# Grouped attention in a 12-layer float32 decoder: dividing the probabilities before their turn, and value products with the values as weights

## The reference, cut to what matters

```python
def _L1_attn_ref(hidden_states, Wq, Wk, Wv, Wo):
    q = (hidden_states @ Wq.T).reshape(B, S, 16, 64).transpose(0, 2, 1, 3)
    k = (hidden_states @ Wk.T).reshape(B, S, 4, 64).transpose(0, 2, 1, 3)
    v = (hidden_states @ Wv.T).reshape(B, S, 4, 64).transpose(0, 2, 1, 3)
    k, v = jnp.repeat(k, 4, axis=1), jnp.repeat(v, 4, axis=1)
    scores = jnp.einsum('bhqd,bhkd->bhqk', q, k) * 64 ** -0.5
    scores = scores + causal[None, None]
    probs = jax.nn.softmax(scores, axis=-1)
    out = jnp.einsum('bhqk,bhkd->bhqd', probs, v)
    return out.transpose(0, 2, 1, 3).reshape(B, S, 16 * 64) @ Wo.T
...
x = _layernorm(x + _L1_attn_ref(x, L1_attn_Wq, L1_attn_Wk, L1_attn_Wv, L1_attn_Wo), axis=-1)
```

## Time and profile before

| | us |
|---|---|
| Median of 3 runs (lowest, highest) | 4686.77 (4686.62, 4692.56) |
| The profiled execution, its own time | 4658.31 |
| Its span | 4656.5 |
| TensorE, VectorE busy | 3992.7, 3324.2 |
| ScalarE, GpSimd busy | 2208.0, 1392.6 |
| First fill to last aggregate of the L1a stage | 1331.2 to 1987.2 |

### The profile page before, as it was taken

One profiled execution on the slowest core, in us unless ns is written; L12 is line 12 of the kernel. 1 busy time (PEld: TensorE's weight loads), 2 busy tenths in 40 slices (PEclk: granted clock), 3 DMA queues, 4 the chain that ended last, 5 costly groups with the idle time before them and its releaser, 6 DMA issues. The chain is left out here.

```text
span 4656.5 us, 142989 instructions
## 1 busy us (share of the span) xinstructions
PE 3992.7 (86%) x51849; PEld 2927.6 (63%) x51890; DVE 3324.2 (71%) x7831; ACT 2208.0 (47%) x3967; POOL 1392.6 (30%) x2469
## 2 busy tenths in 40 slices
PE   8997997999989999889899561799998968879986
PEld 6775666565667877767677441577675434447765
DVE  7986883555557777678788316788786767759985
ACT  4554552222224344356588133455784345545543
POOL 5653341000000000012245505233222234435543
PEclk9998996999999999999999585899998978889998
DMA  2011111000000000011000252000111200000001
GB/s 72 27 46 36 38 36 35 11 14 10 10 13 1 0 0 0 1 41 44 29 17 17 66 149 63 12 13 13 32 33 43 57 7 0 0 12 23 23 17 36
DMA packets 184580, 127.91 MB, mean 27 GB/s; under 512 B 43056, under 2 KB 175408, under 8 KB 184112
## 3 DMA queue, kind: packets, MB, share of 16 engines
q1 hardware_dynamic: 168128, 110.62, 8.0%
q0 software_dynamic: 4096, 8.40, 0.6%
q10 hardware_dynamic: 12144, 6.03, 0.4%
HBM read 77.24 MB, written 18.35 MB: 21 GB/s over the span
## 5 line engine op out<-in xcount | busy, mean ns | idle before, releaser
L920 DVE TENSOR_TENSOR L0f_SG<-L0f_SG,L0f_psY 128x512 f32<-128x512 f32 x176 | 120.6, 685 | 219.5 <-PE L0f_psY L849 219.0
L888 ACT ACTIVATE L0f_SG<-L0f_psY 128x512 f32<-128x512 f32 x176 | 105.1, 597 | 357.1 <-PE L0f_psY L847 357.1
L860 PEld LDWEIGHTS L0f_psO<-L0f_W,L0f_G 128*128 128x128 f32 x1408 | 182.2, 191 | 101.5 <-issue 61.9
L860 PE MATMUL L0f_psO<-L0f_W,L0f_G 128*128 128x128 f32 x1408 | 188.3, 277 | 17.1 <-DVE L0f_G L924 10.9
L2351 POOL TENSOR_TENSOR L1a_rs<-L1a_ag,eps 128x1 f32<-128x1 f32 x64 | 12.1, 189 | 593.9 <-DVE L1a_ag L2521 593.9
L847 PE MATMUL L0f_psY<-L0f_XT,L0f_W 128*128 128x512 f32 x352 | 182.1, 599 | 0.7 <-ACT L0f_G3T L876 0.7
L849 PE MATMUL L0f_psY<-L0f_XT,L0f_W 128*128 128x512 f32 x352 | 180.6, 595 | 2.3 <-issue 0.2
L1531 POOL TENSOR_TENSOR L0f_rt<-L0f_ag,eps 128x4 f32<-128x4 f32 x16 | 3.2, 200 | 513.5 <-DVE L0f_ag L1525 513.5
L2461 ACT ACTIVATE L1a_PR<-L1a_PR 128x1024 f32<-128x1024 f32 x64 | 67.6, 1056 | 150.5 <-DVE L1a_PR L2482 150.5
L2443 PE MATMUL L1a_psO<-L1a_WO,L1a_OT 128*128 128x128 f32 x1024 | 133.7, 285 | 2.9 <-DVE L1a_OT L2497 2.6
L2443 PEld LDWEIGHTS L1a_psO<-L1a_WO,L1a_OT 128*128 128x128 f32 x1024 | 122.3, 196 | 20.0 <-issue 16.8
(11 more groups left out here) (647 smaller groups left out, 12914.8 us busy)
## 6 DMA issues: line engine op xcount, KB each, us to landing
L1m_WB<-in_w12b SPq DMA_DIRECT2D x23, 321.0 KB, 3.3
L1m_BUF<-sorted_x SPq DMA_DIRECT2D x23, 256.0 KB, 3.6
sorted_y<-L1m_BUF ACTq DMA_DIRECT2D x23, 256.0 KB, 3.8
L0a_CS<-in_ctx SPq DMA_DIRECT2D x32, 128.0 KB, 2.1
KB<-L0a_KT SPq DMA_DIRECT2D x128, 32.0 KB, 1.8
L0x_CS<-in_ctx SPq DMA_DIRECT2D x32, 128.0 KB, 2.1
L0x_CR<-in_ctxT SPq DMA_DIRECT2D x32, 128.0 KB, 2.3
KB<-L0x_KT SPq DMA_DIRECT2D x128, 32.0 KB, 1.8
```

Of the source, the lines that this page charges most:

```text
L860: m = nc.tensor.matmul(psO[:, j, :], G[:, gb, 0, j * P:(j + 1) * P], W2[:, k, :], start=k == 0 and j == 0, stop=k == NCH - 1, skip_group_c ...
L888: nc.scalar.activation(SG[:, yb, :], psY[:, yb, 0, :], ACT.Silu).then_inc(S["silu"].sem, 1)
L920: nc.vector.tensor_tensor(SG[:, yb, :], SG[:, yb, :], psY[:, yb, 1, :], ALU.mult).then_inc(S["product"].sem, 1)
```

## The change

The probabilities are divided by their sum on VectorE, in place, right behind the reciprocal (new `nc.vector.tensor_tensor` on PR). Their turn waits for that and moves on TensorE from the front of the slot to behind the scores and the fills of place 0; the value products move behind place 1. In them the values are the weights now and the turned probabilities of four heads stream, 256 columns at a time; each sequence s has a PSUM bank, and the result has features on partitions, which is what the projection needs. So ON, its multiplication and its turn are gone, and OT is copied straight from psQ, one sequence by ScalarE, the other by VectorE. Head pairs of the second sequence lie the other way round on partitions, so WO is loaded a second time with its halves swapped. The projection is done for each sequence by itself: 16 matmuls on 64 columns of the array instead of 8 on 128. A line near the top advances counters of the first stage's semaphores.

```diff
                             nc.vector.tensor_scalar(MF[:, M.u, :], MI[:, M.u, :], 0.0, None, ALU.not_equal).then_inc(S["mask_used"].sem, 1)
...
+            S.advance(dict(rows_rest=16 * MORE, weights_rest=32), arrive)
             S.advance(dict.fromkeys(("xs", "rstd", "var_eps", "out_rows", "f_tx", "f_k", "f_q", "f_v", "o_tx", "o_k", "o_q", "o_v"), PAIRS))
             S.advance(dict.fromkeys(("scores", "shifted", "maxed", "probs", "pt_a", "pt_b", "turned_a", "turned_b", "pv", "normed",
                                      "recip", "ot", "o_turned", "proj", "res", "bn", "stats"), TILES))
...
-            WO = mem.sb("WO", [P, QC, D])
+            WO = mem.sb("WO", [P, 2, QC, D])
...
             PR, PT = mem.sb("PR", [P, 2, HEADS, SEQ]), mem.sb("PT", [P, QC, P])
...
-            ON, OT = mem.sb("ON", [P, QC, P]), mem.sb("OT", [P, QC, P])
+            OT = mem.sb("OT", [P, 2, QC, SEQ])
...
             psP, psO = mem.pb("psP", [P, 2, 4, P]), mem.pb("psO", [P, 2, 4, P])
             psJ = psO[:, 0, 0, :]
-            psH = psO.rearrange("p r c (e d) -> p r (c e) d", d=GD)
+            psQ = psO.rearrange("p s c (e q) -> p s (c e) q", q=SEQ)
...
-                    for d, s_ in ((WQ[:, :, :], io["wq"]), (WK[:, :, :], io["wk"]), (WV[:, :, :, :], io["wv"]), (WO[:, :, :], io["wo"])):
+                    for d, s_ in ((WQ[:, :, :], io["wq"]), (WK[:, :, :], io["wk"]), (WV[:, :, :, :], io["wv"]), (WO[:, 0, :, :], io["wo"]), (WO[0:64, 1, :, :], io["wo"][64:128]), (WO[64:128, 1, :, :], io["wo"][0:64])):
                         sp.dma_start(d, s_).then_inc(S["weights_in"].sem, 16)
-                    sp.wait_ge(S["weights_in"].sem, S["weights_in"].base + 64)
-            S.advance(dict(weights_in=64))
+                    sp.wait_ge(S["weights_in"].sem, S["weights_in"].base + 96)
+            S.advance(dict(weights_in=96))
...
             def copy_out(eng, N, n):
...
                     def slot(T):
                         A = T - 1
-                        if A.ok:
-                            pe.wait_ge(S["probs"].sem, S["probs"].base + A.t + 1)
-                            for hb, free, done in ((0, S["ot_a"], S["turned_a"]), (1, S["ot_b"], S["turned_b"])):
-                                if after(A.t):
-                                    pe.wait_ge(free.sem, free.base + A.t)
-                                for j in range(4):
-                                    b = hb * 4 + j
-                                    m = nc.tensor.transpose(psP[:, hb, j, :], PR[:, A.par, 2 * b:2 * b + 2, :].rearrange("p h k -> p (h k)"), ident)
-                                m.then_inc(done.sem, 1)
                         if T.ok:
...
                             copied(pe, T.p, NFILL - 1)
...
                         fills(T, 0)
                         if A.ok:
...
+                            pe.wait_ge(S["normed"].sem, S["normed"].base + A.t + 1)
+                            for hb, free, done in ((0, S["pt_a"], S["turned_a"]), (1, S["pt_b"], S["turned_b"])):
+                                if after(A.t):
+                                    pe.wait_ge(free.sem, free.base + A.t)
+                                for j in range(4):
+                                    b = hb * 4 + j
+                                    m = nc.tensor.transpose(psP[:, hb, j, :], PR[:, A.par, 2 * b:2 * b + 2, :].rearrange("p h k -> p (h k)"), ident)
+                                m.then_inc(done.sem, 1)
+                        fills(T, 1)
+                        if A.ok:
                             pe.wait_ge(S["pt_a"].sem, S["pt_a"].base + A.t + 1)
                             pe.wait_ge(S["pt_b"].sem, S["pt_b"].base + A.t + 1)
                             if after(A.t):
                                 pe.wait_ge(S["res"].sem, S["res"].base + A.t)
                             pace(pe, S)
-                            for c in range(QC):
-                                for r in range(2):
-                                    half_ = slice(64 * r, 64 * r + 64)
-                                    for s in range(2):
-                                        m = nc.tensor.matmul(psH[64 * s:64 * s + 64, r, c, :], PT[half_, c, 64 * s:64 * s + 64],
-                                                             VT[half_, A.u, 2 * A.par + s, c // 4, :], start=True, stop=True)
+                            for g4 in range(2):
+                                for s in range(2):
+                                    for r in range(2):
+                                        half_, o = slice(64 * r, 64 * r + 64), r if s == 0 else 1 - r
+                                        m = nc.tensor.matmul(psQ[64 * o:64 * o + 64, s, 4 * g4:4 * g4 + 4, :], VT[half_, A.u, 2 * A.par + s, g4, :],
+                                                             PT[half_, 4 * g4:4 * g4 + 4, 64 * s:64 * s + 64], start=True, stop=True)
                             m.then_inc(S["pv"].sem, 1)
-                        fills(T, 1)
-                        if A.ok:
-                            pe.wait_ge(S["normed"].sem, S["normed"].base + A.t + 1)
-                            for hb, done in ((0, S["o_turned_a"]), (1, S["o_turned_b"])):
-                                for j in range(4):
-                                    m = nc.tensor.transpose(psP[:, hb, j, :], ON[:, 4 * hb + j, :], ident)
-                                m.then_inc(done.sem, 1)
                         fills(T, 2)
                         if A.ok:
                             pe.wait_ge(S["ot_a"].sem, S["ot_a"].base + A.t + 1)
                             pe.wait_ge(S["ot_b"].sem, S["ot_b"].base + A.t + 1)
                             for c in range(QC):
-                                m = nc.tensor.matmul(psJ, OT[:, c, :], WO[:, c, :], start=c == 0, stop=c == QC - 1)
+                                for s in range(2):
+                                    m = nc.tensor.matmul(psJ[64 * s:64 * s + 64, :], OT[:, s, c, :], WO[:, s, c, :], start=c == 0, stop=c == QC - 1, skip_group_check=True)
                             m.then_inc(S["proj"].sem, 1)
...
                             nc.scalar.activation(PR[:, T.par], PR[:, T.par], ACT.Exp, scale=scale).then_inc(S["probs"].sem, 1)
                         copies(act, T, 1)
                         if A.ok:
-                            act.wait_ge(S["o_turned_a"].sem, S["o_turned_a"].base + A.t + 1)
+                            act.wait_ge(S["pv"].sem, S["pv"].base + A.t + 1)
                             if after(A.t):
                                 act.wait_ge(S["proj"].sem, S["proj"].base + A.t)
-                            nc.scalar.activation(OT[:, 0:4, :], psP[:, 0], ACT.Copy).then_inc(S["ot_a"].sem, 1)
+                            nc.scalar.activation(OT[:, 0, :, :], psQ[:, 0], ACT.Copy).then_inc(S["ot_a"].sem, 1)
                         copies(act, T, 2)
...
                             nc.vector.tensor_tensor(PR[:, T.par].rearrange("p (c r) k -> p r c k", r=2), psS[:, :, :, :],
                                                     mx[:, T.par, :].rearrange("p (r c) -> p r c", r=2).unsqueeze(3).to_broadcast([P, 2, QC, SEQ]), ALU.subtract).then_inc(S["shifted"].sem, 1)
                         copies(dv, T, 0)
+                        copies(dv, T, 1)
                         if A.ok:
                             dv.wait_ge(S["pv"].sem, S["pv"].base + A.t + 1)
-                            dv.wait_ge(S["recip"].sem, S["recip"].base + A.t + 1)
-                            if after(A.t):
-                                dv.wait_ge(S["o_turned_b"].sem, S["o_turned_b"].base + A.t)
-                            nc.vector.tensor_tensor(ON[:, :, :].rearrange("p c (r d) -> p r c d", d=GD), psH,
-                                                    rden[:, A.par, 1, :].rearrange("p (c r) -> p r c", r=2).unsqueeze(3).to_broadcast([P, 2, QC, GD]), ALU.mult).then_inc(S["normed"].sem, 1)
-                        copies(dv, T, 1)
-                        if A.ok:
-                            dv.wait_ge(S["o_turned_b"].sem, S["o_turned_b"].base + A.t + 1)
                             if after(A.t):
                                 dv.wait_ge(S["proj"].sem, S["proj"].base + A.t)
-                            nc.vector.tensor_copy(OT[:, 4:8, :], psP[:, 1]).then_inc(S["ot_b"].sem, 1)
+                            nc.vector.tensor_copy(OT[:, 1, :, :], psQ[:, 1]).then_inc(S["ot_b"].sem, 1)
                         copies(dv, T, 2)
                         if T.ok:
...
                             nc.vector.tensor_reduce(rden[:, T.par, 0, :], PR[:, T.par], AX, ALU.add).then_inc(S["summed"].sem, 1)
                             dv.wait_ge(S["summed"].sem, S["summed"].base + T.t + 1)
                             nc.vector.reciprocal(rden[:, T.par, 1, :], rden[:, T.par, 0, :]).then_inc(S["recip"].sem, 1)
+                            dv.wait_ge(S["recip"].sem, S["recip"].base + T.t + 1)
```

(3 more changed lines are left out.)

## The result

| | median us | ratio to before, same chip |
|---|---|---|
| before | 4686.62 | |
| changed | 4700.15 | **1.0027** (95%: 1.0018 to 1.0036) |

13.5 us slower, where 4694 was forecast: inside the range and inside the likeliest case's own 4683 to 4706. At 0.27% it is just over the 0.2% that the forecast had called no change, a part of that case to which it gave a chance of 0.04. Measured again on another chip, the ratio was 1.0032 (1.0022 to 1.0043).

A forecast was written before the change was run, and what follows sets the result against it. TensorE's order was taken to bound the attention stage, 19.96 us a pair. Work and waits -20 us and clock falls +27 made +7: 4665 in the profiled execution's terms, 4694 with 28 us added for the runs' median; range 4662 to 4724.

The forecast's parts named there:

- likeliest case: Whole kernel: 10 to 18 clock falls of 1.6 to 2.2 us in the attention stage, 4683 to 4706 us; chance 0.42.
- thin stretches: Even slots, scores' end to K fill: about 4.0 us in which TensorE only turns ten blocks, 1.4 us busy.
- Work removed and swapped: Attention pair: ON's turn and waits gone, 3.0 us; value products 1.0 a block, projection 2.04, multiplication 1215 ns on probabilities.
- The X fill's wait: Even slot, TensorE waiting for GpSimd's XS copy behind VectorE's longer chain: 1.6 us where it was 0.4.
- The K fill's wait: Even slot, TensorE waiting for XT, which ScalarE copies behind both PT copies: a new wait of 1.1 us.
- Work and waits in the stage: Attention stage: pairs 19.4 us instead of 19.96, 17 us, plus 5 at the end: -22 us.
- The clock: Even slots of attention: clock falls in about 45 to 50% of pairs, 14 of 30, 1.9 us each, +27 us.
- The copies of WO: In front of the attention stage: two more copies of half of WO, 1.9 us, once, not covered.
- B: Attention stage: the clock holds, under 5 falls, leaving the gain of 20 us, 4666 us; chance 0.33.
- C: Attention stage: the clock falls in nearly every pair, 30 x 1.9 - 20 = +37, 4724 us; chance 0.13.
- D: Value products lose their overlap, both row halves writing one PSUM bank: 2.0 us a block, +44, 4731 us; chance 0.12.

The follow-up runs named there:

- XS early: The changed kernel with GpSimd's XS copy one slot earlier, in front of the wait for the aggregate: 0.9840 of the kernel before, 4581 us.
- XT first: The changed kernel with only ScalarE's XT copy moved in front of the two PT copies, XS staying late: 0.9861 of the kernel before.

## Why the prediction was right, point by point

Both new waits, their sizes and the clock's falls behind about half of the thin stretches are as forecast. That the stage's own sum came out almost exact is luck: it was 5 us longer by the forecast (-22 by work and waits, +27 by the clock) and is 4.9 longer, but the two terms are -31.5 and +36.

- **Work removed and swapped.** The turn of ON went. Value products 1.02 us a block (1.0 said), projection 1.90 (2.04 said, 0.14 too dear), multiplication 1225 ns (1215 said).
- **The X fill's wait**: 1.6 us said, 1.64 measured. VectorE's chain 4.2 said, 4.31 measured. The step said that the wait came from that chain's new 1.1 us and from the turn gone from the front; without the division 1.13 us are left. Only 0.5 us is the division's, since behind it the aggregate is held by the projection. The size was right, the reason only in part.
- **The K fill's wait**: 1.1 said, 1.03 measured.
- **Work and waits in the stage**: -22 us said (17 in the pairs, 5 at the end). With the clock held by added matmuls it is -31.5: a pair takes 19.3 us where it took 19.9, 19 us in 30 pairs, and the end, from the last X fill on, 40.0 where it took 51.7, 12 us. The end is the term that was too small. The sum left out that the old kernel's own two falls there, which the prediction itself prices at 2.6 and 1.6 us, would go with the waits that made them. For the whole kernel -20 us said and -20 measured (0.9957, interval -28 to -12) agree only because of what the start and the stages behind give back.
- **The clock.** 14 falls of 1.9 us, +27, were said. There were 17, and they cost 2.1 us each, 36 us. Taking the share of the pairs by the stretch's place between 3.3 and 4.76 us gave 45 to 50%; it was 17 in 30, 57%. Over the experiments the share does rise with the stretch: none of 30 at 2.3 us (XS early) or 2.8 us (XT first), 7 at 3.5 (without the division), 17 at 4.0. But inside the changed kernel length doesn't tell the stretches apart: all but the first are 3.96 to 4.12 us long, and in the steady part the clock falls behind three of five, in the same order throughout, with some that keep it no shorter than those that lose it. What decides there is open, so that the share came out near is in part luck too.
- **The copies of WO** in front of the stage: 1.9 us said, 4.0 measured in both profiles of the changed kernel. The rate of the four copies before didn't hold for six: the two pieces of 64 partitions took 6.9 us to land.
- **Not foreseen**: the stage behind (L1x), untouched, took 320.7 and 320.6 us in the two profiles of the changed kernel, 317.4 and 317.9 in the two of the old one. Its clock is low for 27 us instead of 21. That is at most a part of it: with the four matmuls added its clock is low for 21 us, and it still takes 319.6. The cause is open. In sum: 4.9 (stage) + 4.0 (copies) + 3.3 (behind) + 1.3 (L1f, not seen again in the second profile) = 13.5 us, the other stages, which differ by up to 1.3 us, left out. So the step from the +7 that was forecast to +13.5 is the copies, 2 us, and the two stages behind, 4.6, which the forecast had at nothing; it isn't the clock.
- **Rivals.** B (the clock holds) is what the kernel with added matmuls shows, not the changed one. C (nearly every pair) is out: 17 of 30. D (no overlap of the value products) is out: both row halves write one bank of psO at 1.02 us a block, as fast as the old form on two banks; its 16 instructions start in groups of four, 0.02 us from first to last, and 0.2 to 0.3 us from group to group. The Trainium skill, TensorEngine Tiling (Array Packing), Gotcha 1: PSUM Pressure, says that different row tiles cannot access one bank at the same time; on different partitions of it the measurement shows no cost, and it decides. The other rule of the Trainium skill, TensorE: Matmul & The Clock Gate, Part 4: PE-mode transpose, that a transpose doesn't count as TensorE being busy in the same way, is contradicted for the clock by the stretch filled with turns, where 3 of the 17 falls were left.

## What to carry to other kernels

When a step is moved on one engine, lay out what stands in front of each wait anew: here a turn that had hidden a GpSimd copy and a ScalarE copy moved behind both, and what is a 2.3% gain with two copies issued earlier was a 0.3% loss without. A wait on TensorE costs more than its length where it makes a stretch thin, since the clock may fall behind it; the granted clock of the stage and the duration of the first matmuls behind a wait show that, and work put into the wait tells it apart from the wait itself. A copy that only reads should not stand behind another tile's wait on an in-order engine.

## What the runs showed of the hardware that was not expected

- Behind a stretch of about 4.0 us with 1.4 us of transposes in it the clock fell in 17 of 30 pairs, to a granted 0.50 (1.2 GHz), for 2.1 us of lost time each; with 1.0 us of matmuls more in the same stretch, never; with 1.0 us of transposes more, in 3.
- The loss is in the rows right behind the wait: K fills of 2.08 us instead of 1.13, while the 32 recorded instructions of the projection, 5.4 us after the K fill's start, were at full speed (1.97 us).
- The two pieces of a weight on 64 partitions each (256 KB) took 6.9 us to land (median) behind 1.25 MB, longer than the whole weight (512 KB) in front of them with 5.2. How much of that is the queue in front and how much the form isn't shown.
